# Four of 32 input products of the state scan on GpSimd, their decays in place in PSUM

## The reference

```python
dt, Bm, Cm = jnp.split(xdbl, [DT_RANK, DT_RANK + D_STATE], axis=-1)
dt = jax.nn.softplus(jnp.einsum('nlr,dr->nld', dt, dt_proj_w) + dt_proj_b)
A = -jnp.exp(A_log)
dA = jnp.exp(dt[..., None] * A)
dBx = dt[..., None] * Bm[:, :, None, :] * xc[..., None]
def step(h, inp):
    a, b, c = inp
    h = a * h + b
    return (h, jnp.sum(h * c[:, None, :], axis=-1))
```

## Time and profile before

| | |
|---|---|
| median of 3 runs | 10,832.1 us (10,815.46 to 10,833.55) |
| time of the profiled execution | 10,800.28 us |
| its span | 10,798.5 us |
| DVE busy, share of the span | 8,935.9 us, 83% |
| PE busy | 8,564.2 us, 79% |
| ACT busy | 6,274.0 us, 58% |
| POOL busy | 6,010.2 us, 56% |

### The profile page before, as it was taken

One profiled execution on the slowest core, in us unless ns is written; L12 is line 12 of the kernel. 1 busy time (PEld: TensorE's weight loads), 2 busy tenths in 40 slices (PEclk: granted clock), 3 DMA queues, 4 the chain that ended last, 5 costly groups with the idle time before them and its releaser, 6 DMA issues. The chain is left out here.

```text
span 10798.5 us, 196681 instructions
## 1 busy us (share of the span) xinstructions
PE 8564.2 (79%) x61658; PEld 3676.9 (34%) x61658; DVE 8935.9 (83%) x10968; ACT 6274.0 (58%) x11797; POOL 6010.2 (56%) x3646
## 2 busy tenths in 40 slices
PE   6888888888888888677777777777777777778860
PEld 3555555555555555222222222222222222222210
DVE  6677777666677776799999999999999999999984
ACT  5666666666666666555555555555555555555543
POOL 2222222222222222678787877878787887887760
PEclk9999999999999999889898988898888888898875
DMA  2222222232222222111111111111111111111119
GB/s 66 67 67 67 67 67 67 72 73 68 67 67 67 67 67 67 42 33 40 33 40 33 38 34 35 38 32 40 33 39 34 36 37 32 40 32 38 35 44 267
DMA packets 855791, 591.00 MB, mean 55 GB/s; under 512 B 621424, under 2 KB 725872, under 8 KB 848464
## 3 DMA queue, kind: packets, MB, share of 16 engines
q1 hardware_dynamic: 751440, 423.61, 16.9%
q0 software_dynamic: 49152, 100.76, 2.5%
q10 hardware_dynamic: 54016, 51.91, 1.5%
HBM read 109.27 MB, written 103.81 MB: 20 GB/s over the span
## 5 line engine op out<-in xcount | busy, mean ns | idle before, releaser
L1161 POOL TENSOR_TENSOR b_hh<-b_hh,b_cn 128x1024 f32<-128x1024 f32 x1600 | 3834.0, 2413 | 1040.3 <-DVE b_hh L1416 1040.2
L1416 DVE TENSOR_TENSOR_SCAN b_hh<-b_dA,b_ub 128x512 f32<-128x512 f32 x3200 | 3864.9, 1208 | 0.0
L1285 ACT ACTIVATE b_dA<-b_db,b_negA 128x448 f32<-128x448 f32 x3200 | 1980.4, 634 | 1723.8 <-PE b_db L1510 1717.9
L270 POOL DMA_DIRECT2D kvsel<-kv x1536 | 1104.3, 721 | 3054.7 <-issue 2409.3
L1408 DVE TENSOR_TENSOR b_ub<-b_ub,b_bn 128x512 f32<-128x512 f32 x3200 | 2175.0, 680 | 358.2 <-PE b_ub L1510 338.2
L1510 PE MATMUL b_ub<-b_rows,b_pick 96*64 96x512 bf16 x6400 | 1398.4, 438 | 1004.3 <-DVE b_hh L1416 954.0
L1510 PEld LDWEIGHTS b_ub<-b_rows,b_pick 96*64 96x64 bf16 x6400 | 357.9, 110 | 3177.7 <-DVE b_hh L1416 2520.3
L1510 PE MATMUL b_db<-b_rows,b_pick 96*64 96x512 bf16 x6400 | 1253.5, 414 | 221.0 <-ACT b_dA L1285 217.9
L546 DVE SCALAR_TENSOR_TENSOR oacc<-vpad,vec,oacc 128x1064 f32<-128x1064 f32 (+1 forms) x934 | 1199.1, 1301 | 11.4
L1546 PE MATMUL b_acc<-b_hh,b_gather 64*32 64x512 f32 x12800 | 1047.4, 717 | 2.8 <-POOL b_hh L1161 2.8
L387 ACT ACTIVATE prob<-score,nmax 128x256 f32<-128x256 f32 (+1 forms) x1600 | 736.1, 474 | 283.5 <-DVE nmax L517 193.2
(11 more groups left out here) (180 smaller groups left out, 12310.6 us busy)
## 6 DMA issues: line engine op xcount, KB each, us to landing
b_rows<-b_term SPq DMA_DIRECT2D x2400, 64.0 KB, 2.0
kvsel<-kv SPq DMA_DIRECT2D x1600, 64.0 KB, 2.0
kvsel<-kv POOLq DMA_DIRECT2D x1536, 64.0 KB, 2.0
xpad<-in_x SPq DMA_DIRECT2D x18, 1568.0 KB, 10.7
ys<-ysb ACTq DMA_DIRECT2D x16, 1600.0 KB, 8.4
b_yc<-ys SPq DMA_DIRECT2D x100, 256.0 KB, 2.7
xr<-b_xo SPq DMA_DIRECT2D x100, 256.0 KB, 2.7
x<-x3pad SPq DMA_DIRECT2D x16, 1568.0 KB, 18.1
```

What stands on the lines that cost most here:

```text
L270: eng.dma_start(kvsel[:, slot, j, :, WPIX * t:WPIX * (t + 1)].unsqueeze(1), kv[:, bass.ds(at[t], 1), :, :]).then_inc((s_kv, s_kg)[j][slot] ...
L1161: nc.gpsimd.tensor_tensor(out=now, in0=now, in1=cn[:, par, :].unsqueeze(1).broadcast_to([C, 2, HT]), op=ALU.mult).then_inc(s_pm, 1)
L1285: nc.scalar.activation(later(dA[:, k % DEEP, :]), later(db[k % 2][:, :]), ACT.Exp, scale=negA[:, 8 * q + e:8 * q + e + 1]).then_inc(s_a, 1)
L1416: nc.vector.tensor_tensor_scan(hh[:, k // 2 % PDEEP, HT * (k % 2):HT * (k % 2 + 1)], dA[:, k % DEEP, :], ub[(UNITS * par + k) % 3][:, :], ...
```

## The change

Of the 32 units of a chunk, four (21, 24, 27 and 30, in `AHEAD`) go another way:

- PE repeats u into `db` and dt into `ub`: the two repeats change places.
- ACT, where the unit's `decay` stood, copies u from `db` into a new SBUF buffer `su` with two places. The copy of the unit 27 waits for the scan of the unit 21, that of 30 for the scan of 24, and so on round.
- POOL multiplies this place of `su` by B (`states_in` on POOL), for unit 21 ahead of the pair 8, for 24 ahead of pair 9, for 27 ahead of pair 11, for 30 ahead of pair 12.
- ACT, five units later in its list, writes a zero over the first token of each sequence in `ub` (128x64 numbers) and takes the exponential in place there (`decay_in_place`).
- DVE does no product for these units. Its scan reads the decays from PSUM and the products from `su`.
- SP: the copies of the rows into `rows` wait for both repeats instead of one.

The diff, without its added blank lines:

```diff
--- before.py
+++ after.py
@@ -941,6 +941,12 @@
         DECAYS_AT = {3: (7, 8), 4: (9,), 5: (10,), 7: (11,), 9: (12,), 10: (13, 14), 11: (15, 16), 12: (17, 18),
                      13: (19, 20)}
 
+        AHEAD = (21, 24, 27, 30)
+        PLAIN = UNITS - len(AHEAD)
         acc = ctx.enter_context(nc.psum_tensor("b_acc", [C, TOK], FP32))
         ub = [bank(f"ub{i}") for i in range(3)]
         db = [bank(f"db{i}") for i in range(2)]
@@ -986,6 +992,7 @@
         cn = sb("cn", [C, PARS, HT])
         dA = sb("dA", [C, DEEP, HT])
         hh = sb("hh", [C, PDEEP, 2 * HT])
+        su = sb("su", [C, 2, HT])
         ym = sb("ym", [C, T, C])
         xo = sb("xo", [C, G, CPX])
 
@@ -1019,6 +1026,8 @@
         s_a = sem("a")
         s_bk = sem("bk")
         s_sc = sem("sc")
+        s_ex = sem("ex")
+        s_sb = sem("sb")
         s_pm = sem("pm")
         s_y = sem("y")
         s_yd = sem("yd")
@@ -1047,6 +1056,19 @@
 
             return ONE + UNITS * n + k + 1
 
+        def plain(n, k):
+            q, r = divmod(k, UNITS)
+            return ONE + PLAIN * n + PLAIN * q + len([x for x in range(r + 1) if x not in AHEAD])
+        def ahead(n, k):
+            return ONE + len(AHEAD) * n + AHEAD.index(k) + 1
+        def own(k):
+            return su[:, AHEAD.index(k) % 2, :]
         def pair(n, j):
             return ONE + PAIRS * n + j + 1
 
@@ -1069,6 +1091,10 @@
         def later(x):
 
             return x.rearrange("c (m t) -> c m t", t=T)[:, :, 1:T]
+        def first_of(x):
+            return x.rearrange("c (m t) -> c m t", t=T)[:, :, 0:1]
 
         block = ctx.enter_context(nc.Block())
 
@@ -1099,7 +1125,8 @@
                 for r, ready in enumerate((s_hi[x], s_mid[x], s_lo[x])):
                     sp.wait_ge(ready, ONE + n + 1)
                     if r == 0 and not is_first(n):
-                        sp.wait_ge((s_dr, s_ur)[x], ONE + UNITS * n - UNITS)
+                        sp.wait_ge(s_dr, ONE + UNITS * n - UNITS)
+                        sp.wait_ge(s_ur, ONE + UNITS * n - UNITS)
                     for q in range(Q):
                         sp.dma_start(rows[32 * r:32 * r + 32, x, par, q, :], terms[x][r][32 * q:32 * q + 32, :]
                                      ).then_inc(s_rows[x], 16)
@@ -1161,6 +1188,12 @@
                 nc.gpsimd.tensor_tensor(out=now, in0=now, in1=cn[:, par, :].unsqueeze(1).broadcast_to([C, 2, HT]),
                                         op=ALU.mult).then_inc(s_pm, 1)
 
+            def states_in(n, par, k):
+                pool.wait_ge(s_a, unit(n, k))
+                pool.wait_ge(s_bn, ONE + 2 * n + 1)
+                nc.gpsimd.tensor_tensor(out=own(k), in0=own(k), in1=bn[:, par, :], op=ALU.mult).then_inc(s_sb, 1)
             inputs(0, 0)
             for x in range(2):
                 left(x, 0)
@@ -1170,6 +1203,9 @@
             def body(n, par):
                 more = before_end(n, 1)
                 for j in range(PAIRS):
+                    for k in AHEAD:
+                        if (k - 5) // 2 == j:
+                            states_in(n, par, k)
                     products(n, par, j)
                     if j == 4 and more:
                         inputs(n + 1, (par + 1) % 3)
@@ -1264,7 +1300,9 @@
 
                 act.wait_ge(s_bp, ONE + 2 * n + x + 1)
                 if not early(n, 3):
-                    act.wait_ge((s_bk, s_pm)[x], ONE + (UNITS, PAIRS)[x] * n - 2 * (UNITS, PAIRS)[x])
+                    act.wait_ge((s_bk, s_pm)[x], ONE + (PLAIN, PAIRS)[x] * n - 2 * (PLAIN, PAIRS)[x])
+                    if x == 0:
+                        act.wait_ge(s_sb, ONE + len(AHEAD) * n - 2 * len(AHEAD))
                 nc.scalar.activation((bn, cn)[x][:, par, :], misc[:, :], ACT.Copy).then_inc(s_bn, 1)
 
             def high(x, n):
@@ -1279,11 +1317,28 @@
 
             def decay(n, k):
                 act.wait_ge(s_dr, unit(n, k))
+                if k in AHEAD:
+                    i = AHEAD.index(k)
+                    if i >= 2:
+                        act.wait_ge(s_sc, unit(n, AHEAD[i - 2]))
+                    elif not is_first(n):
+                        act.wait_ge(s_sc, unit(n - 1, AHEAD[i - 2]))
+                    nc.scalar.activation(own(k), db[k % 2][:, :], ACT.Copy).then_inc(s_a, 1)
+                    return
                 if not (is_first(n) and k < DEEP):
                     act.wait_ge(s_sc, unit(n, k - DEEP))
                 q, e = channel(k)
                 nc.scalar.activation(later(dA[:, k % DEEP, :]), later(db[k % 2][:, :]), ACT.Exp,
                                      scale=negA[:, 8 * q + e:8 * q + e + 1]).then_inc(s_a, 1)
+            def decay_in_place(n, par, k):
+                act.wait_ge(s_ur, unit(n, k))
+                q, e = channel(k)
+                here = ub[(UNITS * par + k) % 3][:, :]
+                nc.scalar.activation(first_of(here), first_of(dA[:, 0, :]), ACT.Copy)
+                nc.scalar.activation(later(here), later(here), ACT.Exp, scale=negA[:, 8 * q + e:8 * q + e + 1]
+                                     ).then_inc(s_ex, 1)
 
             def evac(n):
                 act.wait_ge(s_o, ONE + n + 1)
@@ -1355,6 +1410,7 @@
                     kept(n + 1, nxt, 1)
                 decay(n, 25)
                 decay(n, 26)
+                decay_in_place(n, par, 21)
                 if more:
                     middle(1, n + 1)
                 decay(n, 27)
@@ -1362,10 +1418,19 @@
                     reorder(n + 2)
                 for k in range(28, 32):
                     decay(n, k)
+                    if k == 29:
+                        decay_in_place(n, par, 24)
                 if before_end(n, 2):
                     turned(n + 2)
                 if more:
-                    for k in range(UNITS, UNITS + LEAD):
+                    decay(n, UNITS)
+                decay_in_place(n, par, 27)
+                if more:
+                    for k in range(UNITS + 1, UNITS + 4):
+                        decay(n, k)
+                decay_in_place(n, par, 30)
+                if more:
+                    for k in range(UNITS + 4, UNITS + LEAD):
                         decay(n, k)
 
             chunks(act, body)
@@ -1409,13 +1474,19 @@
                                         ).then_inc(s_bk, 1)
 
             def recur(n, par, k):
-                dve.wait_ge(s_bk, unit(n, k))
-                dve.wait_ge(s_a, unit(n, k))
+                here = ub[(UNITS * par + k) % 3][:, :]
+                if k in AHEAD:
+                    dve.wait_ge(s_ex, ahead(n, k))
+                    dve.wait_ge(s_sb, ahead(n, k))
+                    rate, new = here, own(k)
+                else:
+                    dve.wait_ge(s_bk, plain(n, k))
+                    dve.wait_ge(s_a, unit(n, k))
+                    rate, new = dA[:, k % DEEP, :], here
                 if k % 4 == 0 and not (is_first(n) and k // 2 < PDEEP):
                     dve.wait_ge(s_y, quad(n, (k // 2 - PDEEP) // 2))
-                nc.vector.tensor_tensor_scan(hh[:, k // 2 % PDEEP, HT * (k % 2):HT * (k % 2 + 1)], dA[:, k % DEEP, :],
-                                             ub[(UNITS * par + k) % 3][:, :], 0.0, ALU.mult, ALU.add
-                                             ).then_inc(s_sc, 1)
+                nc.vector.tensor_tensor_scan(hh[:, k // 2 % PDEEP, HT * (k % 2):HT * (k % 2 + 1)], rate, new, 0.0,
+                                             ALU.mult, ALU.add).then_inc(s_sc, 1)
 
             front(0)
             states_in(0, 0, 0)
@@ -1423,7 +1494,7 @@
             def body(n, par):
                 more = before_end(n, 1)
                 for k in range(UNITS):
-                    if k + 1 < UNITS or more:
+                    if k + 1 not in AHEAD and (k + 1 < UNITS or more):
                         states_in(n, par, k + 1)
                     recur(n, par, k)
                     if k == 8 and not is_first(n):
@@ -1516,7 +1587,7 @@
                     pe.wait_ge(s_rows[1], ONE + 192 * n + 192 * (k // UNITS) + 192)
                 if not (is_first(n) and k < 3):
                     pe.wait_ge(s_sc, unit(n, k - 3))
-                repeat(ub[(UNITS * par + k) % 3], 1, par, k, s_ur)
+                repeat(ub[(UNITS * par + k) % 3], 0 if k in AHEAD else 1, par, k, s_ur)
 
             def repeat_dt(n, par, k):
                 if k % UNITS == 0:
@@ -1527,7 +1598,7 @@
                     pe.wait_ge(s_ze, ONE + 2 * n + 3)
                 if k == 8 and before_end(n, 1):
                     pe.wait_ge(s_xe, ONE + 2 * n + 4)
-                repeat(db[k % 2], 0, par, k, s_dr)
+                repeat(db[k % 2], 1 if k in AHEAD else 0, par, k, s_dr)
 
             def skip(n, par, h):
                 if h == 0 and not is_first(n):
```

## The result

| | before | after |
|---|---|---|
| median of the runs | 10,823.8 us (4 runs, 10,805.9 to 10,833.6) | 11,028.4 us (4 runs, 11,018.9 to 11,035.4) |
| profiled execution | 10,800.3 us | 11,018.9 us |
| DVE busy | 8,935.9 us | 8,706.5 us |
| POOL busy | 6,010.2 us | 6,491.2 us |

The ratio is 1.019, with a 95% interval of 1.0172 to 1.0208: slower by 1.9%, against a forecast of 11,017 us for the median.

A forecast was written before the change was run, and what follows sets the result against it. DVE was taken to set the pace. Per chunk, +3.33 us wait at unit 21, -1.74 saved and +0.3 for PE gave +1.89, together +185 us: 11,017 us for the median, range 10,900 to 11,160.

The forecast's parts named there:

- The wait at unit 21: DVE's scan of unit 21 waits for POOL's late product, starting 3.33 us later per chunk in the mean.
- What is saved: Scans of 24, 27 and 30 each lose a 0.58 us DVE product ahead of them: 1.74 us a chunk.
- The decays in place: ACT's work between the scans of 21 and 24: 3.35 us against 3.42 due, just in time.
- PE term: PE's repeats and matmuls crowded behind unit 21's scan: +0.3 us a chunk, ends -0.7 and +1.74.
- The low end: PE catches up during unit 21's pause in 20 of 83 chunks: PE term -0.7 us, total 10,920 us.
- a rival that the clock is then at 2.4 GHz more often: The pause at unit 21 pays, all ends low at once: about the same, 10,850 us; chance 0.03.
- The sum: Per chunk +3.33 - 1.74 + 0.3 = +1.89 us, 99 times; together +185 us, 11,017 for the median.
- POOL is not late: Rival: unit 21's product on POOL is ready in time, four times 0.58 us saved, 10,600 us; chance 0.06.
- turning point: POOL's lateness at unit 21 of 1.74 us, where the three other savings are used up.
- PE or ACT takes the savings back: Rival: savings behind unit 21 are lost too, about 330 us more, 11,160 us; chance 0.12.
- POOL and DVE slow each other: Rival: POOL's four new products each up to 0.89 us longer beside DVE, about 11,350 us; chance 0.02.

The follow-up runs named there:

- e3: Changed kernel with POOL's products of 21 and 24 ahead of pair 9, 27 ahead of 11, 30 ahead of 12: 11,265.7 us, ratio 1.041.
- e1: Changed kernel with POOL's products moved forward: unit 21 ahead of pair 6, 24 of 7, 27 of 9, 30 of 10: 10,718.3 us, ratio 0.9909.
- e10: Changed kernel with only the product of unit 21 moved forward on POOL, ahead of pair 6: 10,977.2 us, ratio 1.0179.
- e7: As e4, with POOL's products of pairs 7 to 12 cut to 8 of 512 columns (output incomplete): 10,899.2 us, ratio 1.0081.
- e4: Changed kernel with the four units' products with B done by DVE in SBUF instead of by POOL: 11,292.6 us, ratio 1.0436.
- e5: As e1, with su four places wide, each copy waiting only for the last chunk's scan of its own unit: 10,699.6 us, ratio 0.9889.
- e9: Kernel before the change, with PE's transposes and convolution for the chunk after next moved from units 26-30 to 22-26, ACT's work along: 10,812.8 us, ratio 1.0025.
- e11: As e6, with PE's work for the chunk after next behind units 22-26, ACT's work moved along, middle(1) behind PE's awaited copy: 10,831.1 us, ratio 1.0015.
- e6: Changed kernel with four su places, units 15, 18, 21, 27, POOL's products ahead of pairs 5, 5, 6, 8, decays moved to match: 10,679.5 us, ratio 0.9879.

## Why the prediction was right

- **The wait at unit 21.** Forecast: DVE idle 3.6 us in most chunks and up to 4.4, some 385 us in sum. Measured: about 3.7 us in 67 of 99 chunks and up to 4.49, 387.8 us in sum, with POOL's `b_su` as releaser. The product that I priced at 1.2 us took 1.27. e3 (later by a pair: +2.4 us of wait a chunk), e1 (forward: wait gone) and e10 (the wait goes to the next unit) show that the order on POOL's list makes it. That a delay is not made up in the next chunk was right too.
- **What is saved.** 400 products less, 229.4 us of DVE's busy time, against 232 worked out. The scans of 24, 27 and 30 did not wait for POOL: the 99 waits, 3.92 us in the mean, are all at unit 21.
- **The decays in place.** Forecast: 3.35 us of ACT's work in 3.42, just in time. They were: no scan of the change waited for one. The exponential took 0.60 us where I took 0.63 from the row, so the Trainium skill's statement that ScalarE reaches PSUM faster ("ScalarE: Activation LUTs", Step-by-step: what each stage is for) is borne out by 0.03 us. In e7 the whole path costs nothing that can be measured.
- **The PE term was too small.** I took +0.3 us a chunk; the page gives 71.8 / 99 = 0.7. Behind unit 21 the waits rose from 0.63 to 2.1 us a chunk, and at the units 0 to 8 they fell from 2.38 to 1.67. The low end had assumed that the pause at unit 21 lets PE catch up, and a rival that the clock is then at 2.4 GHz more often. The clock did the opposite. Here are PE's last repeats ahead of its pause of 4.86 us and the first behind it, then three windows (PE, PEld, DVE, ACT, POOL busy, clock, DMA):

```profile
8032.34 0.41 PE L1581 MATMUL b_ub<-b_rows,b_pick 96*64 96x512 bf16 x2 [0.49 <-DVE b_hh L1488]
8032.58 0.38 PE L1581 MATMUL b_db<-b_rows,b_pick 96*64 96x512 bf16 x2
8037.83 0.64 PE L1581 MATMUL b_ub<-b_rows,b_pick 96*64 96x512 bf16 x2 [4.86 <-DVE b_hh L1488]
```

```profile
8031.00:8033.00 2.00, 1.41 (x16) 0.40 (x8) 1.88 (x3) 1.51 (x3) 2.00 (x1) 1.00 0.41 98
8037.80:8049.60 11.80, 11.34 (x44) 2.98 (x44) 8.89 (x10) 6.66 (x13) 11.80 (x8) 0.51 0.18 45
8049.60:8053.00 3.40, 3.40 (x31) 0.90 (x30) 3.22 (x5) 1.71 (x4) 3.40 (x2) 1.00 0.00 0
```

  Ahead of the pause the granted clock is 1.00 (2.4 GHz) and a pair of repeats takes 0.38 to 0.41 us. Behind it the clock is at half (1.2 GHz), a pair takes 0.64, and PE is busy 11.34 of the next 11.80 us. So it is at all 98 pauses of PE of 3.5 us and more in this stage: the granted clock is 1.00 ahead of each and 0.50 behind it. From 28 to 36 us behind the gate, where this stretch lies, the mean granted clock over the chunks is 0.54, where the kernel before has 0.77 and e1, without the pause, 0.70. What part of the PE term this is stays open: e1 has no pause, and its waits behind unit 21 are 2.2 us a chunk.
- **The sum.** 3.33 - 1.74 + 0.3 = 1.89 us a chunk was forecast, +185 us in all; the stage took 231 us more. The PE term alone was 42 us too small (71.8 against 30), the two other terms 5 us. That the forecast for the median came within 11 us is luck in part: the first stage ran 11 us faster in the profiled execution after the change, and I had added 32 us from the profiled execution to the median, where it is 9.5 after the change. The medians lie 205 us apart.
- **The rivals.** "POOL is not late" had 1.74 us of lateness as its turning point; e1, which removes the lateness, is indeed on the other side, but reaches 10,718 and not the 10,600 worked out for this case, since DVE's waits for PE take back 140 of the 232 us. "PE or ACT takes the savings back" came true in part, by PE alone. "POOL and DVE slow each other" did not occur in the change: its scans took 1.21 us on average and POOL's pairs 2.41, as before. e4 made it occur.

What stays open is what exactly sets DVE's waits for PE. e5 rules out the copies, e9 and e11 show that moving PE's work only moves the waits or adds to them, and in both a lower granted clock goes with it. No run holds the clock fixed, so whether it causes these waits is not shown.

## What to carry to other kernels

An engine that is busy 56% of the time can still be late at one place in its list. Before giving it work that a bottleneck will wait for, read in its timeline when it gets there, and compare that with when the result is due. Here the same work, placed 7 to 9 us sooner in the list, turned a loss of 1.9% into a gain of 0.9%. With other units and more buffer places the gain was 1.2%, a difference that the intervals do not quite separate.

## What the runs showed of the hardware that was not expected

- A DVE product with both inputs in SBUF, begun during a POOL instruction that reads SBUF, took 2.60 us instead of 0.66: it ended 0.55 us after that instruction's end (e4). I had expected up to 0.9 us more for each; that was the mean, and a single product lost up to 2.0.
- The new wait of DVE makes PE pause once a chunk, and PE came out of 98 such pauses at half the granted clock that it had gone in with. In the chunk shown the pause is 4.86 us and the clock stays at half for 11.8 us behind it, of which PE is busy 11.34.
- With PE's work for the chunk after next moved forward by four units, PE's mean granted clock between 5,400 and 10,200 us was 0.85 in e11, against 0.89 in e6, and the kernel was slower. That the one causes the other is not shown.
